# Silu in halves and two gates at earlier places in a four-layer Mamba stage

## The chip, the cores and the metric

One core of one Trainium2 chip. The metric is device microseconds of one execution of the whole kernel. Three runs of the kernel before gave 6634.72, 6636.77 and 6638.04 us, median 6636.77.

## The reference, cut to what matters

The kernel is a chain of eight stages: self-attention, cross-attention, feed-forward, a Mamba stage, a norm, cross-attention, feed-forward and a last attention. Only the Mamba stage is changed. It works on 8 sequences of 576 positions (64 of a prefix, 512 of the input) with 256 channels, in four layers of this block:

```
xi, z = split(x @ ip_w.T, 2)                  # 512 channels each
xi = silu(causal depthwise conv of 4 taps(xi) + cb)
dt, Bm, Cm = split(xi @ xp_w.T, [16, 32])     # 16 + 16 + 16
dt = softplus(dt @ dtp_w.T + dtp_b)
dA = exp(dt * A);  dBu = dt * Bm * xi         # 512 channels x 16 states
h = dA * h + dBu  (over the positions);  y = sum over states of h * Cm
y = (y + xi * D) * silu(z)
out = y @ op_w.T  (+ residual)
```

## The kernel before, in words

The 8 x 576 positions are one row of 4608, cut into 9 chunks of 512. Four layers of 9 chunks make 36 **steps** (a loop over 2 of 18 bodies; N is the body, c the chunk). A step scans 512 channels x 16 states = 8192 rows, 128 at a time: 64 **units** (i = 0 to 63) of 128 x 512, two to a **pair** (j = 0 to 31), eight pairs to a channel group k of 128 channels.

What each engine does for a pair, every one in a program order written out by hand:

- POOL (GpSimd) makes the fed product u * B for both units (line 2506). For ten pairs (0, 5, 8, 11, 14, 16, 20, 24, 26, 28) it also multiplies the scanned state with C (line 2511), three pairs later. After pair 26 and pair 31 it makes dt * xi for the next step (line 2252) and writes a reset value (line 2255).
- ACT (ScalarE) saves the last state column of pair j - 2 (line 2133, or line 2129 for a pair of POOL's), once that pair's PSUM slots have been read, and then writes exp(dt * A) into the slots (line 2474). There are four slots, two pairs.
- DVE (VectorE) scans each unit (line 2429) and, for the 22 pairs that POOL does not take, multiplies with C, one instruction for each unit (line 2237).
- PE (TensorE) folds the states of a pair into the bank of its channel group (line 2384), and signals `summed`.

Between these stand the pieces that prepare the next step, each at a fixed unit or pair: on PE the conv-and-input projections of channel groups 0 to 3 at pairs (23, 25), (27, 28), (30, 31) and, one step on, (2, 3) (project_x, line 1992), the output projection at pairs 5 and 6 (lines 2032 to 2043), the mean square at pair 7 (line 2018), the x projection at pairs 10 and 11 (line 2052), dt at 15 and 19, z at 13, 21, 24, 29 (line 2010). On ACT the copies out of PSUM, Square behind unit 5 (line 2205), silu of all of z behind unit 7 (lines 2168 and 2169), bias of group 3 behind unit 13 (line 2161), silu of all of xi behind unit 15 (lines 2173 and 2174), residual copies behind units 18 and 19 (lines 2146 and 2143), Ln and Exp of the norm behind 21 and 23 (lines 2208, 2211), softplus behind 37 and 45. Each silu is a load of the silu table, one 128 x 2048 activation, and a load of the exp table. On DVE the **gates**, y * silu(z) for one channel group (line 2232): group 3 of the step before ahead of unit 7, groups 0, 1, 2 ahead of units 23, 39 and 55. Gate k waits for `summed` of pair 8k + 7.

PE comes to a piece or a fold only after all that stands ahead of it. DVE comes to the scan of a unit only after the gate that stands ahead of it. The four lines that set the places:

```
E_OUT, G_OUT, F_OUT, SILU_AT = (59, 3, 9, 13), 29, (55, 49, 33, 1), (15, 7)
SQUARE_AT, RSTD_AT, SCALE_AT = 5, (21, 23), 26
for f in range(KI - 1):
    if i == 16 * (f + 1) + 7: gate(e, N, f, z[:, n % 2])
```

Of the kernel before, what the change touches and what calls it, by code (L numbers as in the profile page):

```python
# [18 lines left out]
ALU = mybir.AluOpType  # L19
ACT = mybir.ActivationFunctionType  # L20
# [1803 lines left out]
def load_first(e, core, layer):  # L1824

    e.dma_start(core.weights[1][:, CONV_AT:CONV_AT + TAPS * KD * DI], layer_of(core.taps, layer)).then_inc(core.first_loaded, 16)
    e.dma_start(layer_vec(core, "norm", "conv_b"), vec_from(core, layer, "norm", "conv_b")).then_inc(core.first_loaded, 16)
# [44 lines left out]
def val(N, per, off):  # L1872

    l, j = N
    return l * (BODIES * per) + (j * per + off)
# [14 lines left out]
def v_at(N, name):  # L1890

    return BEFORE_V[name] + 1 if N[1] == -2 else val(N, len(LANE_V), V_BASE + LANE_V[name] + 1)


def s_at(N, name):

    return BEFORE_S[name] + 1 if N[1] == -2 else val(N, len(LANE_S), S_BASE + LANE_S[name] + 1)
# [12 lines left out]
def mamba(core):  # L1910
    at = 0
    ring, at = core.area(at, RING, 2, TC)
# [5 lines left out]
    u, at = core.area(at, KI, TC)  # L1918
# [59 lines left out]
    def reset_of(c):  # L1978

        return 64 * (c % CHUNKS) if c % CHUNKS < B else None  # L1980
# [40 lines left out]
    def late_pe(e, N, j, c, xi, nb, gone):  # L2021

        if j == E_AT[3][0]:
            e.wait_ge(ln.v_free, v_before(N, "E3"))
        for half in range(2):
            if j == E_AT[3][half]:
                project_x(e, 3, half, c + 1, lane_v, nb, ln.v_full)
        if j == PE_B[1]:
            if N[1] >= 0:
                e.wait_ge(gated, gated_at(previous(N), KI - 1))  # L2030
            if N[1] >= 0:
                e.matmul(ybank[1], core.ident[:], chunk(c + CHUNKS - 1)[:, 1, :], start=True, stop=False)
                for k in range(KI):
                    mm = e.matmul(ybank[1], out_w[:, k, P:D], gone[:, k, :], start=False, stop=(k == KI - 1))
            else:
                mm = e.matmul(ybank[1][:, 0:2], core.ident[:], core.ident[:, 0:2], start=True, stop=True)
            mm.then_inc(y_full, 1)
        if j == PE_B[0]:
            e.wait_ge(ln.s_free, s_before(N, "B0"))
            if N[1] >= 0:  # L2040
                e.matmul(lane_s, core.ident[:], chunk(c + CHUNKS - 1)[:, 0, :], start=True, stop=False)
                for k in range(KI):
                    mm = e.matmul(lane_s, out_w[:, k, 0:P], gone[:, k, :], start=False, stop=(k == KI - 1))
            else:
                mm = e.matmul(lane_s[:, 0:2], core.ident[:], core.ident[:, 0:2], start=True, stop=True)
            mm.then_inc(ln.s_full, 1)
        if j == G_AT[0]:
            e.wait_ge(ln.s_free, s_before(N, "G"))
            e.wait_ge(silu, val(N, 2, 4))
        if j in G_AT:  # L2050
            for k in (0, 1) if j == G_AT[0] else (2, 3):
                mm = e.matmul(lane_s[0:48, :], x_w[:, k, :], xi[:, k, :], start=(k == 0), stop=(k == KI - 1))
            if j == G_AT[1]:
                mm.then_inc(ln.s_full, 1)
        for pair in range(2):
            if j == PE_H[pair]:
                project_dt(e, N, pair)
        if j == PE_F[2]:
            if N[1] >= 0:
                e.wait_ge(gated, gated_at(N, 0))  # L2060
            project_z(e, N, 2, ybank[0], nb).then_inc(y_full, 1)
        if j == PE_F[1]:
            if N[1] >= 0:
                e.wait_ge(gated, gated_at(N, 1))
            else:
                e.wait_ge(y_added, 1)
            project_z(e, N, 1, ybank[1], nb).then_inc(y_full, 1)
        if j == PE_F[0]:
            e.wait_ge(ln.v_free, v_before(N, "F0"))
            project_z(e, N, 0, lane_v, nb).then_inc(ln.v_full, 1)  # L2070
        if j == PE_F[3]:
            if N[1] >= 0:
                e.wait_ge(gated, gated_at(N, 2))
            else:
                e.wait_ge(y_free, 1)
            project_z(e, N, 3, ybank[0], nb).then_inc(y_full, 1)
# [29 lines left out]
            e.wait_ge(y_free, y_free_at(N, "F1"))  # L2106
        e.matmul(ybank[k % 2], diag[:, k, :], xi[:, k, :], start=True, stop=False)

    E_OUT, G_OUT, F_OUT, SILU_AT = (59, 3, 9, 13), 29, (55, 49, 33, 1), (15, 7)
    H_OUT = (37, 45)  # L2110

    def soft_plus(e, N, pair):
# [35 lines left out]
    def late_act(e, N, n, i, c, xi, zi, zn):  # L2148

        if i == F_OUT[3] and N[1] >= 0:  # L2150
            e.wait_ge(y_full, y_at(previous(N), "F3"))
            e.activation(zn[:, 3, :], ybank[0], ACT.Copy).then_inc(y_free, 1)
        if i == E_OUT[1]:
            e.wait_ge(ln.v_full, v_at(previous(N), "E1"))
            e.activation(xi[:, 1, :], lane_v, ACT.Identity, bias=lv("conv_b", 1)).then_inc(ln.v_free, 1)
        if i == E_OUT[2]:
            e.wait_ge(ln.s_full, s_at(previous(N), "E2"))
            e.activation(xi[:, 2, :], lane_s, ACT.Identity, bias=lv("conv_b", 2)).then_inc(ln.s_free, 1)
        if i == E_OUT[3]:
            e.wait_ge(ln.v_full, v_at(N, "E3"))  # L2160
            e.activation(xi[:, 3, :], lane_v, ACT.Identity, bias=lv("conv_b", 3)).then_inc(ln.v_free, 1)
        if i == SILU_AT[1]:
            if N[1] >= 0:
                e.wait_ge(y_free, y_free_at(N, "F3"))
                e.wait_ge(ln.v_free, v_at(previous(N), "F0"))
            else:
                e.wait_ge(cleared, 1)
            e.activation(zn, zn, ACT.Silu).then_inc(silu, 1)
            e.preload_act_table_set("natural_log_exp_and_others")
        if i == SILU_AT[0]:  # L2170
            e.wait_ge(ln.v_free, v_at(N, "E3"))
            e.wait_ge(ln.s_free, s_at(previous(N), "E2"))
            e.activation(xi, xi, ACT.Silu).then_inc(silu, 1)
            e.preload_act_table_set("natural_log_exp_and_others")
        for m in range(KD):
            if i == RESIDUAL[m]:
                residual(e, N, m, c)
        if i == G_OUT:
            e.wait_ge(ln.s_full, s_at(N, "G"))
            if N[1] >= 0:  # L2180
                e.wait_ge(bc_stored, val(N, 16, 16))
            e.activation(xdbl[0:48, :], lane_s[0:48, :], ACT.Copy).then_inc(ln.s_free, 1)
        for pair in range(2):
            if i == H_OUT[pair]:
                e.preload_act_table_set("softplus")
                soft_plus(e, N, pair)
                e.preload_act_table_set("natural_log_exp_and_others")
        if i == F_OUT[2]:
            e.wait_ge(y_full, y_at(N, "F2"))
            e.activation(zi[:, 2, :], ybank[0], ACT.Copy).then_inc(y_free, 1)  # L2190
        if i == F_OUT[1]:
            e.wait_ge(y_full, y_at(N, "F1"))
            e.activation(zi[:, 1, :], ybank[1], ACT.Copy).then_inc(y_free, 1)
        if i == F_OUT[0]:
            e.wait_ge(ln.v_full, v_at(N, "F0"))
            e.activation(zi[:, 0, :], lane_v, ACT.Copy).then_inc(ln.v_free, 1)

    SQUARE_AT, RSTD_AT, SCALE_AT = 5, (21, 23), 26

    def early_act(e, N, i, c, xe, nb, nb_before):  # L2200

# [25 lines left out]
    def gate(e, N, k, zi):  # L2227

        e.wait_ge(summed, summed_at(N, SP_ * (k + 1) - 1))
        if k == 0:  # L2230
            e.wait_ge(silu, val(N, 2, 3))
        e.tensor_tensor(zi[:, k, :], ybank[k % 2], zi[:, k, :], ALU.mult).then_inc(gated, 1)

    def times_c(e, N, n, j, h):
# [12 lines left out]
    def times_x(e, N, pair, xi, c):  # L2247

        e.wait_ge(ln.s_free, s_at(N, ("H0", "H3")[pair]))
        e.wait_ge(ln.v_free, v_at(N, ("H1", "H2")[pair]))  # L2250
        at = slice(2 * pair, 2 * pair + 2)
        e.tensor_tensor(u[:, at, :], dt[:, at, :], xi[:, at, :], ALU.mult).then_inc(u_done, 1)
        e.wait_ge(u_done, u_done_at(N, pair, 1))
        p = reset_of(c)
        e.tensor_tensor(scrap[:, 12:14] if p is None else dt[:, at, p], far, core.one[:, 0:2], ALU.mult).then_inc(u_done, 1)

    def build_diag(e):

# [26 lines left out]
    with core.nc.Block() as block:  # L2285
        @block.sync
        def _(e):
# [12 lines left out]
            for l in range(LAYERS // 2):  # L2300
                for j in range(BODIES):
# [9 lines left out]
                    spread_dt(e, 2)  # L2311
                    spread_u(e, 2)
                    if c == CHUNKS - 2:
                        load_first(e, core, after)
                    store_bc(e, N, (j + 1) % 2)
                    e.wait_ge(scanned, scanned_at(N, 31))
# [77 lines left out]
        def _(e):  # L2394
# [15 lines left out]
            for l in range(LAYERS // 2):  # L2410
                for n in range(BODIES):
                    N, c = (l, n), n % CHUNKS
                    layer = l * 2 + n // CHUNKS
                    for i in range(UN):
# [3 lines left out]
                            e.wait_ge(core.first_loaded, layer * FIRST_LOAD + 2 * FIRST_LOAD)  # L2418
                        early_dve(e, N, i, c, normed[:, n % 2])
                        for f in range(KI - 1):  # L2420
                            if i == 16 * (f + 1) + 7:
                                gate(e, N, f, z[:, n % 2])
                        if i == 7:
                            gate(e, previous(N), KI - 1, z[:, (n + 1) % 2])
# [404 lines left out]
```

## Time and profile before

| | |
|---|---|
| median of 3 runs | 6636.77 us |
| profiled execution, its time / its span | 6639.8 / 6638.0 us |
| Mamba scans, first to last | 2054.0 to 5993.9 us of the span |
| busy share of the span: PE, DVE, ACT, POOL | 92%, 74%, 55%, 66% |
| mean granted TensorE clock | 0.941 |

Read it like this: the shares are means over eight stages. In the Mamba stage, 59% of the span, DVE's row of the slices shows 9 in every slice, POOL's too, PE's 8 or 9 and ACT's 6. The page's chain of work that ended last covers only the last stages, so the Mamba stage is read from timelines.

### The profile page before, as it was taken

The numbers are of one execution on the slowest core, as the hardware profiler recorded it, in microseconds if no ns is written. First come the engines' busy times: TensorE is split into PE (matmuls) and PEld (weight loads), VectorE is DVE, ScalarE is ACT, GpSimd is POOL, SyncE is SP. The second block draws the span as 40 slices with busy tenths as digits, with TensorE's granted clock in tenths as the row PEclk, the third lists the DMA queues.
The fourth block names the chain that finished last, engine by engine and source line by source line (L and its number), as shares of the span: only waits on it lengthen the run. The fifth ranks groups of instructions, "written<-read, shape, count | busy, mean of one in ns | idle before, by whom it ended". The sixth has DMA issues, their size and how long they took to land. (4 is left out here: it accounts for less than half of the span.)

```text
span 6638.0 us, 60681 instructions
## 1 busy us (share of the span) xinstructions
PE 6129.0 (92%) x20586; PEld 2577.4 (39%) x20586; DVE 4928.1 (74%) x5709; ACT 3620.5 (55%) x6605; POOL 4394.1 (66%) x2056
## 2 busy tenths in 40 slices
PE   9999999999999989898899989898989898988898
PEld 4555555544443333323333323333323343323444
DVE  4444445543225999999999999999999999995623
ACT  4444445432225666666666666666666666664432
POOL 3333334323005999999999999999999999992300
PEclk9999999999998989899989999999999898989998
DMA  2000000213002333333333333332333232332000
GB/s 80 1 1 1 1 1 1 86 26 102 20 0 68 83 76 78 78 93 85 72 89 71 83 88 86 71 89 65 89 81 93 65 89 65 93 80 56 4 0 26
DMA packets 228678, 387.64 MB, mean 58 GB/s; under 512 B 46304, under 2 KB 64416, under 8 KB 225936
## 3 DMA queue, kind: packets, MB, share of 16 engines
q1 hardware_dynamic: 228368, 383.75, 23.7%
q8 instruction: 164, 2.69, 0.2%
q14 instruction: 146, 1.20, 0.1%
HBM read 207.14 MB, written 23.40 MB: 35 GB/s over the span
## 5 line engine op out<-in xcount | busy, mean ns | idle before, releaser
L2506 POOL TENSOR_TENSOR work<-work,weights 128x1024 f32<-128x1024 f32 x1152 | 2685.6, 2361 | 15.8 <-PE banks L2384 6.8
L2429 DVE TENSOR_TENSOR_SCAN banks<-banks,work 128x512 f32<-128x512 f32 x1584 | 1985.7, 1272 | 53.5 <-ACT banks L2474 48.1
L2384 PE MATMUL banks<-work 128*64 128x512 f32 x4608 | 1353.9, 670 | 378.2 <-POOL work L2511 271.1
L2474 ACT ACTIVATE banks<-work 128x512 f32<-128x512 f32 x2304 | 1496.0, 680 | 25.5
L1992 PE MATMUL banks<-work,weights 128*128 128x512 f32 (+31 forms) x3796 | 1140.6, 451 | 3.0 <-DVE work L2222 3.0
L2237 DVE TENSOR_TENSOR work<-banks,weights 128x512 f32<-128x512 f32 x1584 | 1056.0, 668 | 0.0
L2511 POOL TENSOR_TENSOR work<-work,weights 128x1024 f32<-128x1024 f32 x360 | 848.0, 2356 | 238.4 <-ACT work L2129 238.4
L2429 DVE TENSOR_TENSOR_SCAN work<-banks,work 128x512 f32<-128x512 f32 x720 | 911.2, 1269 | 99.8 <-ACT banks L2474 97.2
L603 POOL TENSOR_TENSOR work<-work 128x1024 f32<-128x1024 f32 x256 | 479.6, 1893 | 743.4 <-DVE work L470 742.9
L1992 PEld LDWEIGHTS banks<-work,weights 128*128 128x128 f32 x3796 | 634.4, 190 | 600.0 <-issue 523.6
L2133 ACT ACTIVATE work<-banks 128x2 f32<-128x2 f32 x792 | 135.9, 172 | 1227.4 <-DVE work L2237 1225.6
L2384 PEld LDWEIGHTS banks<-work 128*64 128x64 f32 x4608 | 271.0, 145 | 1236.4 <-issue 500.8
L553 ACT ACTIVATE work<-banks,work 128x512 f32<-128x512 f32 x512 | 347.7, 690 | 201.1 <-DVE work L464 201.1
L464 DVE TENSOR_REDUCE work<-banks 128x2 f32<-128x1024 f32 x256 | 308.8, 1214 | 105.1 <-PE banks L389 104.7
L2010 PE MATMUL banks<-work,weights 128*128 128x512 f32 x592 | 350.7, 722 | 0.0
L1040 PE MATMUL banks<-work,weights 128*128 128x512 f32 x768 | 341.5, 599 | 9.4 <-ACT work L215 9.4
L454 DVE COPY work<-banks 128x512 f32<-128x512 f32 x256 | 175.5, 685 | 160.3 <-PE banks L379 160.3
L379 PE MATMUL banks<-ident,work 128*128 128x128 f32 x2048 | 277.9, 279 | 8.2 <-DVE work L454 4.6
L379 PEld LDWEIGHTS banks<-ident,work 128*128 128x128 f32 x2048 | 222.1, 141 | 151.7 <-issue 111.1
L389 PE MATMUL banks<-work 64*128 64x512 f32 x1024 | 254.4, 615 | 0.0
L366 PE MATMUL banks<-work 128*64 128x256 f32 x2048 | 247.5, 385 | 0.0
L322 PE MATMUL banks<-work,weights 128*128 128x512 f32 x512 | 224.9, 597 | 6.4 <-ACT work L215 4.2
(312 smaller groups left out, 6796.9 us busy)
## 6 DMA issues: line engine op xcount, KB each, us to landing
weights<-mamba_bc SPq DMA_DIRECT2D x592, 256.0 KB, 5.0
work<-work SPq DMA_DIRECT2D x1160, 128.0 KB, 2.3
weights<-mamba_taps SPq DMA_DIRECT2D x5, 2048.0 KB, 7.5
weights<-cross_vo SPq DMA_DIRECT2D x16, 512.0 KB, 6.9
mamba_taps<-work SPq DMA_DIRECT2D x4, 2048.0 KB, 7.8
cross_vo<-weights SPq DMA_DIRECT2D x6, 1024.0 KB, 8.4
work<-in_conv_rows SPq DMA_DIRECT2D x16, 256.0 KB, 6.7
out_T<-X SPq DMA_DIRECT2D x8, 512.0 KB, 3.3
```

The costliest lines, as they stand in the source:

```text
L379: mm = e.transpose(core.banks[:, 4 + j, kt * P:(kt + 1) * P], probs[:, 2 * (g % 2) + u, j, kt * P:(kt + 1) * P], core.ident[:])
L553: last = e.activation(probs[:, slot, j, :], core.banks[:, 2 * u + j, :], ACT.Exp, bias=nmax[:, slot, j:j + 1], accum_out=sums[:, slot, j:j ...
L603: e.tensor_tensor(probs[:, slot], probs[:, slot], rsum[:, slot, :].unsqueeze(2).to_broadcast([P, 2, T]), ALU.mult) \
L1040: mm = e.matmul(bank(i), w1[:, k, m * P:(m + 1) * P], normed[:, k, :], start=(k == 0), stop=(k == KD - 1))
L1992: mm = e.matmul(lane[:, a:b], conv_w[j][:, k, m * P:(m + 1) * P], nb[:, k, a + j:b + j], start=(d == 0 and k == 0), stop=(j == 0 and b == ...
L2010: mm = e.matmul(lane, z_w[:, k, m * P:(m + 1) * P], nb[:, k, TAPS - 1:], start=(k == 0), stop=(k == KD - 1))
L2237: last = e.tensor_tensor(ring_pair(n, j)[:, h, :], banks[:, slot_of(i), :], bc[:, j % SP_, 1, :], ALU.mult)
L2384: mm = e.matmul(ybank[k % 2][64 * h:64 * h + 64, :], fold, ring_pair(n, j)[:, h, :], start=False, stop=(a == SP_ - 1))
L2429: e.tensor_tensor_scan(ub if by_pool(j) else da, da, ub, state[:, i:i + 1], ALU.mult, ALU.add).then_inc(scanned, 1)
L2474: e.activation(banks[:, slot_of(i), :], dt_rep[:, k % 2, h, :], ACT.Exp, scale=decay[:, f:f + 1]).then_inc(da_full, 1)
L2506: e.tensor_tensor(ring_pair(n, j), u_rep[:, k % 2], bc[:, a, 0, :].unsqueeze(1).to_broadcast([P, 2, TC]), ALU.mult) \
L2511: e.tensor_tensor(ring_pair(n, q), ring_pair(n, q), bc[:, q % SP_, 1, :].unsqueeze(1).to_broadcast([P, 2, TC]), ALU.mult) \
```

## The change

Places of work on ACT and DVE move inside the step; ACT's two silus of 2048 columns become four of 1024. z is done in halves behind units 5 and 27, xi behind units 15 and 21, each half with its own two table loads. The bias of group 3 moves from 13 to 15 (ahead of the first xi half), Ln and Exp from 21 and 23 to 23 and 24. Gates 0 and 1 move from 23 and 39 to 21 and 37; gate 2 stays at 55, and gate 3 at 7. PE's x projection waits for the second xi half. POOL's small reset write is left out where there is no reset (one step in nine). SP waits for the group 3 bias before it loads the next layer's first weights (once a layer). The change's own short title also names VectorE's products with C, "one for each unit"; the diff has no line of `times_c`, which makes one for each unit already.

```diff
@@ late_pe
         if j == G_AT[0]:
             e.wait_ge(ln.s_free, s_before(N, "G"))
-            e.wait_ge(silu, val(N, 2, 4))
+            e.wait_ge(silu, val(N, 4, 7))
@@
-    E_OUT, G_OUT, F_OUT, SILU_AT = (59, 3, 9, 13), 29, (55, 49, 33, 1), (15, 7)
+    E_OUT, G_OUT, F_OUT = (59, 3, 9, 15), 29, (55, 49, 33, 1)
+    Z_SILU, X_SILU = (5, 27), (15, 21)
+    GATE_AT = (21, 37, 55)
@@ late_act
-        if i == SILU_AT[1]:
...
-            e.activation(zn, zn, ACT.Silu).then_inc(silu, 1)
-            e.preload_act_table_set("natural_log_exp_and_others")
-        if i == SILU_AT[0]:
...
-            e.activation(xi, xi, ACT.Silu).then_inc(silu, 1)
-            e.preload_act_table_set("natural_log_exp_and_others")
+        for half in range(2):
+            at = slice(2 * half, 2 * half + 2)
+            if i == Z_SILU[half]:
...
+                e.activation(zn[:, at, :], zn[:, at, :], ACT.Silu).then_inc(silu, 1)
+                e.preload_act_table_set("natural_log_exp_and_others")
+            if i == X_SILU[half]:
...
+                e.activation(xi[:, at, :], xi[:, at, :], ACT.Silu).then_inc(silu, 1)
+                e.preload_act_table_set("natural_log_exp_and_others")
@@
-    SQUARE_AT, RSTD_AT, SCALE_AT = 5, (21, 23), 26
+    SQUARE_AT, RSTD_AT, SCALE_AT = 5, (23, 24), 26
@@ gate
-        if k == 0:
-            e.wait_ge(silu, val(N, 2, 3))
+        if k % 2 == 0:
+            e.wait_ge(silu, val(N, 4, (5, 8)[k // 2]))
@@ times_x
+        p = reset_of(c)
+        e.tensor_tensor(u[:, at, :], dt[:, at, :], xi[:, at, :], ALU.mult).then_inc(u_done, 2 if p is None else 1)
+        if p is None:
+            return
@@ sync
                     if c == CHUNKS - 2:
+                        e.wait_ge(ln.v_free, v_at(N, "E3"))
                         load_first(e, core, after)
@@ vector
-                            if i == 16 * (f + 1) + 7:
+                            if i == GATE_AT[f]:
```

## Rows read from the trace of the kernel before

**Rows 1.** Stretches: length, busy us (x) of PE, PEld, DVE, ACT, POOL, PE clock, DMA.

```profile
3359.00:3408.50 49.50, 49.50 (x171) 23.62 (x171) 46.44 (x51) 34.92 (x60) 44.95 (x21) 1.00 0.46 107
2054.00:5994.00 3940.00, 3561.79 (x10573) 1301.16 (x10571) 3808.31 (x4103) 2535.20 (x4505) 3684.90 (x1662) 0.92 0.35 81
```

**Rows 2.** Waits of DVE, 2070 to 5995 us: total, times, longest.

```profile
DVE work L2429 <- ACT banks L2474: 71.5, 36, 2.4
DVE banks L2429 <- ACT banks L2474: 41.7, 40, 1.2
DVE work L2232 <- PE banks L2384: 4.1, 7, 1.0
```

**Rows 3.** Timeline of DVE: start, us, line; units 41, 6, 8, 16, 21, gate 0, 38, 41.

```profile
3333.61 1.27 DVE L2429 TENSOR_TENSOR_SCAN work<-banks,work 128x512 f32<-128x512 f32 x1
...
3379.87 1.27 DVE L2429 TENSOR_TENSOR_SCAN banks<-banks,work 128x512 f32<-128x512 f32 x1
...
3385.24 1.29 DVE L2429 TENSOR_TENSOR_SCAN banks<-banks,work 128x512 f32<-128x512 f32 x1 [1.14 <-ACT banks L2474]
...
3400.26 1.28 DVE L2429 TENSOR_TENSOR_SCAN work<-banks,work 128x512 f32<-128x512 f32 x1 [1.92 <-ACT banks L2474]
...
3407.95 1.28 DVE L2429 TENSOR_TENSOR_SCAN banks<-banks,work 128x512 f32<-128x512 f32 x1
...
3411.50 0.68 DVE L2232 TENSOR_TENSOR work<-banks,work 128x512 f32<-128x512 f32 x1
...
3436.60 1.29 DVE L2429 TENSOR_TENSOR_SCAN banks<-banks,work 128x512 f32<-128x512 f32 x1
...
3442.53 1.27 DVE L2429 TENSOR_TENSOR_SCAN work<-banks,work 128x512 f32<-128x512 f32 x1
```

**Rows 4.** Timeline of POOL: products with C of pairs 20 and 26.

```profile
3335.43 2.35 POOL L2511 TENSOR_TENSOR work<-work,weights 128x1024 f32<-128x1024 f32 x1 [1.00 <-ACT work L2129]
...
3356.51 2.36 POOL L2511 TENSOR_TENSOR work<-work,weights 128x1024 f32<-128x1024 f32 x1
```

**Rows 5.** Timeline of PE: fold 26, output projection, fold 7.

```profile
3358.92 1.08 PE L2384 MATMUL banks<-work 128*64 128x512 f32 x4 [0.52 <-POOL work L2511]
...
3400.97 3.60 PE L2043 MATMUL banks<-work,weights 128*128 128x512 f32 x8
...
3407.43 1.08 PE L2384 MATMUL banks<-work 128*64 128x512 f32 x4
```

**Rows 6.** Timeline of ACT in the same step.

```profile
3373.84 1.29 ACT L2474 ACTIVATE banks<-work 128x512 f32<-128x512 f32 x2
...
3375.16 1.05 ACT L2205 ACTIVATE work<-X 128x1024 f32<-128x1024 f32 x1
...
3379.73 1.28 ACT L2168 ACT_TABLE_LOAD   x1
3381.02 1.91 ACT L2168 ACTIVATE work<-work 128x2048 f32<-128x2048 f32 x1
...
3384.25 0.17 ACT L2133 ACTIVATE work<-banks 128x2 f32<-128x2 f32 x1
3384.45 1.30 ACT L2474 ACTIVATE banks<-work 128x512 f32<-128x512 f32 x2
...
3392.75 0.69 ACT L2161 ACTIVATE work<-banks,weights 128x512 f32<-128x512 f32 x1 [0.55 <-PE banks L1992]
...
3404.61 0.60 ACT L2143 ACTIVATE X<-banks 128x512 f32<-128x512 f32 x1 [0.45 <-PE banks L2043]
...
3405.20 1.29 ACT L2474 ACTIVATE banks<-work 128x512 f32<-128x512 f32 x2
```

**Rows 7.** Timeline of ACT and PE ahead of the first scan.

```profile
2020.19 0.69 ACT L2161 ACTIVATE work<-banks,weights 128x512 f32<-128x512 f32 x1 [6.17 <-PE banks L1992]
...
2031.06 0.59 ACT L2182 ACTIVATE work<-banks 48x512 f32<-48x512 f32 x1 [4.25 <-PE banks L2052]
...
2025.69 5.33 PE L2052 MATMUL banks<-work,weights 128*48 128x512 f32 x8 [2.78 <-ACT work L2143]
```

More of the change, by code:

```diff
@@ L2161, in late_act @@
             e.activation(xi[:, 3, :], lane_v, ACT.Identity, bias=lv("conv_b", 3)).then_inc(ln.v_free, 1)
-        if i == SILU_AT[1]:
[L2163 to L2167, printed above, removed]
-            e.activation(zn, zn, ACT.Silu).then_inc(silu, 1)
-            e.preload_act_table_set("natural_log_exp_and_others")
-        if i == SILU_AT[0]:
-            e.wait_ge(ln.v_free, v_at(N, "E3"))
-            e.wait_ge(ln.s_free, s_at(previous(N), "E2"))
-            e.activation(xi, xi, ACT.Silu).then_inc(silu, 1)
-            e.preload_act_table_set("natural_log_exp_and_others")
+        for half in range(2):
+            at = slice(2 * half, 2 * half + 2)
+            if i == Z_SILU[half]:
+                if half == 0 and N[1] >= 0:
+                    e.wait_ge(y_free, y_free_at(previous(N), "F1"))
+                    e.wait_ge(ln.v_free, v_at(previous(N), "F0"))
+                if half == 0 and N[1] < 0:
+                    e.wait_ge(cleared, 1)
+                if half == 1 and N[1] >= 0:
+                    e.wait_ge(y_free, y_free_at(N, "F3"))
+                e.activation(zn[:, at, :], zn[:, at, :], ACT.Silu).then_inc(silu, 1)
+                e.preload_act_table_set("natural_log_exp_and_others")
+            if i == X_SILU[half]:
+                if half == 0:
+                    e.wait_ge(ln.v_free, v_at(previous(N), "E1"))
+                else:
+                    e.wait_ge(ln.v_free, v_at(N, "E3"))
+                    e.wait_ge(ln.s_free, s_at(previous(N), "E2"))
+                e.activation(xi[:, at, :], xi[:, at, :], ACT.Silu).then_inc(silu, 1)
+                e.preload_act_table_set("natural_log_exp_and_others")
         for m in range(KD):
@@ L2251, in times_x @@
         at = slice(2 * pair, 2 * pair + 2)
-        e.tensor_tensor(u[:, at, :], dt[:, at, :], xi[:, at, :], ALU.mult).then_inc(u_done, 1)
+        p = reset_of(c)
+        e.tensor_tensor(u[:, at, :], dt[:, at, :], xi[:, at, :], ALU.mult).then_inc(u_done, 2 if p is None else 1)
+        if p is None:
+            return
         e.wait_ge(u_done, u_done_at(N, pair, 1))
-        p = reset_of(c)
-        e.tensor_tensor(scrap[:, 12:14] if p is None else dt[:, at, p], far, core.one[:, 0:2], ALU.mult).then_inc(u_done, 1)
+        e.tensor_tensor(dt[:, at, p], far, core.one[:, 0:2], ALU.mult).then_inc(u_done, 1)
     def build_diag(e):
@@ L2313, in _ @@
                     if c == CHUNKS - 2:
+                        e.wait_ge(ln.v_free, v_at(N, "E3"))
                         load_first(e, core, after)
```

## The prediction, made blind

> **What bounds the kernel now.** I read the busy shares first, then DVE's waits, then the four engines' timelines over one step, because shares hide who waits in which part of it. In the Mamba stage DVE is busy for 3808 of 3940 us, POOL 3685, PE 3562 and ACT 2535 [rows 1]. Nearly all of DVE's idle time is a wait for ACT's exp: 71.5 and 41.7 us [rows 2]. The timeline places it. Behind unit 7 stands the silu of z, and the scan of unit 8 comes 1.22 us late, start against start; behind unit 15 stands the silu of xi, and unit 16 comes 1.99 us late [rows 3]. Both repeat in all 36 steps. The softplus behind unit 37 makes unit 38 late by 0.14 us. Read so, the stage is DVE's work plus about 3.4 us of ACT's stalls in a step of 108.92 us (scan of unit 41 to the same scan a step later [rows 3]).
>
> That isn't the whole loop. Follow PE. The scan of unit 41 starts at 3333.61. ACT saves its state, POOL, which had waited for that, makes the product of pair 20 at 3335.43, and then works without a gap to the product of pair 26, 3356.51 to 3358.87 [rows 3, 4]. PE had waited 0.52 us for this, folds pair 26 at 3358.92, and from there has no idle time at all until the fold of pair 7 ends at 3407.43 + 1.08 = 3408.51 [rows 5]: 49.50 of 49.50 us busy, at a granted clock of 1.00, which is 2.4 GHz, so nothing is left to speed up there [rows 1]. The conv and output projections stand in that run. So PE is some three pairs behind DVE at the start of a step. The end of group 3's projection is what ACT waits for ahead of unit 14 (0.55 us, until 3392.75), and behind that come the exps of pair 7, the xi silu and the late unit 16 [rows 6]. So the long stall at unit 16 is partly PE's lateness, passed on by ACT. The closed loop of today is: unit 41, POOL, PE's run, ACT, unit 16, DVE to unit 41. The trace bears this out: fold 7 ends 0.55 us behind the start of unit 21 in 33 of 36 steps, although the steps' own lengths vary from 108.9 to 114.8 us. In the step shown that is 3408.51 against 3407.95 [rows 3, 5].
>
> **The change, part by part.** All times are those of the step shown.
>
> *z half behind unit 5.* Today the two loads and the silu take 3384.25 - 3379.73 = 4.52 us; the silu itself is 1.91 us. No row shows a silu of 1024 columns. Its bounds are half of 1.91, 0.96, and all of it, 1.91; I take 1.04, the mean of the 1024-column Square [rows 6]. So a half costs 4.52 - 1.91 + 1.04 = 3.65 us. Behind the exps of pair 2 (end 3375.13) it runs to 3378.80, history copy and Square (0.09 + 1.05, now behind it) to 3379.95, the state copy 0.20, and a scan follows its exp's start by 0.79 (3384.45 to 3385.24): unit 6 starts at 3380.94, not 3379.87, 1.07 late. Unit 8 is no longer late: exps follow at once. Net at unit 8: 0.15 us earlier than today.
>
> *Bias and xi half behind unit 15.* The bias no longer stands ahead of the exps of pair 7. These end at about 3393.44, the bias at 3394.13, the half at 3397.78, and unit 16 starts at 3398.77. DVE would be there at 3398.12: 0.65 us late instead of 1.99. Unit 16 comes 1.49 us sooner than today.
>
> *Residual behind unit 19, unchanged.* It waits for PE's output projection, whose end at 3400.97 + 3.60 = 3404.57 the change does not move. Exps of pair 10 start at 3405.20 as today, so unit 20 can't start before 3405.99. DVE, ready at 3404.69, waits 1.3 us. Of the 1.49 us won, 0.19 are left.
>
> *Gate 0 ahead of unit 21.* Today it starts at 3411.50, 2.99 us behind the end of fold 7. Two scans and two products, 3.55 us (3411.50 - 3407.95), are what lies between the old place and the new. There DVE is ready at 3407.76 and fold 7 ends at 3408.51. Gate 0 waits until about 3408.56, 0.61 us later than DVE stands at this point today. Everything behind it on DVE waits too.
>
> *xi half behind unit 21.* The exps of pair 10 end at 3406.49, the half at 3410.16, exp of unit 22 starts at 3410.36, its scan at 3411.15. DVE arrives at 3408.56 + 0.60 + 1.19 + 0.59 = 3410.94: 0.21 late. With 0.96 for the half it would be 0.13, with 1.91 it would be 1.08. Offset against today: 0.61 + 0.21 = 0.82 us. PE's x projection finds this half done by 3407.9, long before fold 9, so its new wait costs nothing.
>
> *Ln and Exp behind 23 and 24, z half behind 27.* The exps of units 24 and 25 are then ready about 0.1 us ahead of their scans: nothing. Behind 27 ACT has its slots early, since pair 11 is POOL's, and between unit 23 and unit 28 DVE has two norm products more: ready some 0.8 us early. Nothing; if that cover goes, the half's excess over DVE's work lands on unit 28.
>
> *Gate 1 ahead of 37.* Its 0.60 us now cover the softplus: unit 38's 0.14 us go [rows 3]. Fold 15 ends at the start of unit 37 in 17 steps (up to 2 us sooner in the others), so it may wait 0.05 there. I book -0.14.
>
> *The rest.* POOL's small write goes in 8 places: under 0.2 us each. SP's wait is over before SP gets there (unit 15's scan, then the bias a few us on): nothing but a later load, used a step and a half on. The products with C are one for each unit already: nothing. The four more table loads and the longer silus, 5.3 us of ACT in a step, otherwise lie in ACT's idle time, (3940 - 2535) / 36 = 39 us a step [rows 1].
>
> *Ahead of the first scan* nothing is hidden. From the end of the group 3 bias at 2020.88: first half 3.65, two tiny copies, table and silu of the second half until 2027.0; the x projection (5.33 us, began at 2025.69) ends at about 2032.4; ACT meanwhile does the second load, Ln, Exp and the last z half until 2033.2, so the copy of dt, B and C starts there and not at 2031.06 [rows 7]. +2.2 us.
>
> **The sum.** In a step 0.82 - 0.14 = +0.68 us, with no other slack in the loop to take it: unit 41 starts later by this, and with it POOL, PE's run and the next gate 0. 36 x 0.68 = 24.5; three steps have fold 7 0.17 to 0.3 us sooner, -0.5; +2.2. In all +26 us: 6666 us against the profiled execution's 6639.8, which lies 3 us above the median; against the median, 6663 us. What this kernel's measurement can tell from no change is about 0.2%, 13 us.
>
> A rule speaks against the change more strongly: every switch of table set costs 2.66 us with its drain, so work should be grouped by set (the Trainium skill, "ScalarE: Activation LUTs", What ACT_TABLE_LOAD costs). The rows disagree on the size, since two loads and the silu between them take 4.52 us in all [rows 6]; by the page the sum would be that of the last rival.
>
> **The rivals.**
>
> *Faster: PE doesn't hold gate 0 or the residual.* If PE's run came along with DVE, only ACT's stalls would count: 1.22 + 1.99 + 0.14 today, 1.07 + 0.65 + about 0.2 changed, 1.4 us less a step, 36 x 1.4 = 51, less 2.2 ahead of the first scan: 6588 us. For it: DVE's waits name ACT for 113 us and PE for 4 [rows 2]. Against it: a run of 49.5 us without idle time that starts from unit 41, and the constant 0.55 us. Chance 0.15.
>
> *Same: the two small terms are smaller.* The ends of matmuls are modelled. If fold 7 is readable 0.3 us sooner and the half is 0.96, the step gains 0.61 - 0.3 + 0.13 - 0.14 = 0.3: 36 x 0.3 + 2.2 = 13 us at most, 6645 us. Against it: gate 3, which waits for fold 31, never starts less than 0.05 us behind its modelled end. Chance 0.14.
>
> *Slower by more: a half-size silu is hardly shorter.* At 1.91 unit 22 is 1.08 late: 36 x 0.87 = 31 us more, 6694 us. It decides from 0.83 us on, where the half outlasts gate, scan and product. Against it: all other ACT rows grow with their columns. Chance 0.04.
>
> *Slower by far: a switch costs twice its load.* Then a half takes 3.65 + 2 x 1.28 = 6.2 us, nearly all of the difference lands on unit 22 and some on unit 16: about +3.2 us a step, 6752 us. This is that page's rule as a mechanism of this kernel. Against it: the 4.52 us. Chance 0.01.
>
> **How the numbers follow.** The forecast, PE-bound gate 0, has 0.66 and its own range is 6652 (no late unit 22) to 6675 (half of 1.3 us). Slower by over 0.2%: 0.66 + 0.04 + 0.01 = 0.71; same 0.14; faster 0.15. The range goes from 6630, which takes in the same case with some gain ahead of it, to 6678; it leaves out the faster rival and the two dear ones, 0.20.
>
> **What the changed profile would show.** DVE's waits name PE ahead of gate 0 in nearly every step, about 0.8 us each, some 25 to 30 us in all against 4.1. ACT's waits remain: about 1.0 at unit 6, 0.6 at 16, 1.2 at 20 (behind the residual, so PE's), 0.2 at 22; none at 8 and 38. The step is 109.6 us, PE's run from fold 26 to fold 7 still 49.6 us without a gap, table loads 8 + 4 a step. I am wrong if gate 0 starts without a wait, if the silu halves differ from 1.04 us, or if PE's run is shorter: then the loop was not through PE.

## The result and the profile after

| | before | changed |
|---|---|---|
| median of 7 runs each | 6636.85 us | 6661.6 us |
| ratio, 95% interval | | 1.004 (1.0028 to 1.0051) |
| profiled execution's span | 6638.0 us | 6664.4 us |
| first scan / last scan start | 2054.0 / 5992.7 us | 2058.2 / 6021.5 us |
| scan of unit 41 to the same a step later, mean of 35 | 109.32 us | 110.01 us |

Slower by 0.4%: +0.69 us a step. One of the seven runs of the kernel before, at 7251.69 us where the others lie between 6632.89 and 6638.04, is left out of the ratio. Lines 2429, 2384, 2232, 2237, 2506, 2511 and 2474 of before are 2441, 2396, 2241, 2246, 2518, 2523 and 2486 now. The first view is again DVE's list of waits over the Mamba stage (total us, times, longest):

```profile
DVE banks L2441 <- ACT banks L2486: 87.0, 71, 1.9
DVE work L2241 <- PE banks L2396: 24.7, 36, 0.7
DVE work L2441 <- ACT banks L2486: 22.3, 37, 1.3
DVE work L2441 <- POOL work L2518: 2.8, 3, 0.9
```

The sum named ACT went from 113 us [rows 2] to 109; what is new is the line with PE, 36 times, once a step. The timeline of DVE in the step that answers to the one shown before (units 6, 16, 20, gate 0, units 21, 22; all starts are 12.26 us later than in that trace, counted at the scan of unit 41 ahead of it, 3345.87 against 3333.61):

```profile
3393.13 1.29 DVE L2441 TENSOR_TENSOR_SCAN banks<-banks,work 128x512 f32<-128x512 f32 x1 [0.91 <-ACT banks L2486]
...
3410.84 1.28 DVE L2441 TENSOR_TENSOR_SCAN work<-banks,work 128x512 f32<-128x512 f32 x1 [0.46 <-ACT banks L2486]
...
3418.26 1.29 DVE L2441 TENSOR_TENSOR_SCAN banks<-banks,work 128x512 f32<-128x512 f32 x1 [1.42 <-ACT banks L2486]
...
3420.83 0.69 DVE L2241 TENSOR_TENSOR work<-banks,work 128x512 f32<-128x512 f32 x1 [0.70 <-PE banks L2396]
3421.43 1.28 DVE L2441 TENSOR_TENSOR_SCAN banks<-banks,work 128x512 f32<-128x512 f32 x1
...
3423.44 1.28 DVE L2441 TENSOR_TENSOR_SCAN work<-banks,work 128x512 f32<-128x512 f32 x1
```

Units 8 and 38 wait no more, unit 16 waits 0.46 where it waited 1.92 [rows 3]. Up to there DVE has won 1.68 us (unit 16 at 3410.84 - 12.26 = 3398.58 against 3400.26). Not all of it is the half silu's. These lines of ACT are the first xi load and the next instruction behind the block, first before, then changed:

```profile
3394.74 1.28 ACT L2173 ACT_TABLE_LOAD   x1
...
3399.26 0.17 ACT L2133 ACTIVATE work<-banks 128x2 f32<-128x2 f32 x1
```

```profile
3406.18 1.28 ACT L2182 ACT_TABLE_LOAD   x1
...
3409.84 0.17 ACT L2135 ACTIVATE work<-banks 128x2 f32<-128x2 f32 x1
```

The block takes 3.66 us instead of 4.52, which is 0.86; and it starts 0.82 us sooner (3406.18 - 12.26 = 3393.92 against 3394.74), because the group 3 bias, which before waits for PE until 3392.75 [rows 6], no longer stands ahead of the exps of pair 7.

Then three waits behind one another, at unit 20, gate 0 and unit 22, take it all back and more. (Unit 22 starts 0.82 us behind the start of the product ahead of it, where 0.59 is usual, so it is 0.23 us late; the view doesn't list idle time that short.) PE and ACT in the same step say why:

```profile
3413.25 3.60 PE L2043 MATMUL banks<-work,weights 128*128 128x512 f32 x8
3416.78 1.08 PE L2396 MATMUL banks<-work 128*64 128x512 f32 x4
3417.78 1.99 PE L2018 MATMUL banks<-work,mean_d 128*128 128x512 f32 x4
3419.70 1.08 PE L2396 MATMUL banks<-work 128*64 128x512 f32 x4
```

```profile
3416.88 0.60 ACT L2145 ACTIVATE X<-banks 128x512 f32<-128x512 f32 x1 [2.15 <-PE banks L2043]
3417.38 0.20 ACT L2131 ACTIVATE work<-work 128x2 f32<-128x2 f32 x1
3417.47 1.29 ACT L2486 ACTIVATE banks<-work 128x512 f32<-128x512 f32 x2
3418.78 1.28 ACT L2182 ACT_TABLE_LOAD   x1
3420.08 1.06 ACT L2182 ACTIVATE work<-work 128x1024 f32<-128x1024 f32 x1
3421.15 1.28 ACT L2183 ACT_TABLE_LOAD   x1
3422.44 0.17 ACT L2135 ACTIVATE work<-banks 128x2 f32<-128x2 f32 x1
```

PE's output projection ends at 3416.85, the residual copy waits 2.15 us for it where it waited 0.45 [rows 6], and behind it come the exps of pair 10, the second xi half, and unit 22. Fold 7 ends at 3419.70 + 1.08 = 3420.78, and gate 0 starts 0.05 us later. In this step PE did nothing else than before: its fold of pair 7 starts 73.83 us behind the scan of unit 41 (3419.70 - 3345.87), 73.82 before (3407.43 - 3333.61, [rows 3, 5]). Over 35 steps the end of fold 7 lies 74.92 us behind that scan in the middle (median), 74.90 before; 30 of the steps agree within 0.05 us, and in five the fold is 0.15 to 0.28 us sooner now. Fold 7 to unit 21 of the same step: unit 21 started 0.55 us ahead of fold 7's end in 33 of 36 steps before, and 0.65 us behind it in all 36 now.

### The profile page after: what moved, and what is told of

Its sections match the earlier page's. It is cut to its first block and busy times, and to the rows that moved or that the text cites. A ratio compares the mean times of both kernels' runs of the same rounds, so it can differ in the third digit from the quotient of the medians.

```text
span 6664.4 us, 60931 instructions
## 1 busy us (share of the span) xinstructions
PE 6131.3 (92%) x20586; PEld 2566.7 (39%) x20586; DVE 4933.8 (74%) x5709; ACT 3821.4 (57%) x6827; POOL 4397.1 (66%) x2048
## 5 line engine op out<-in xcount | busy, mean ns | idle before, releaser
L2396 PE MATMUL banks<-work 128*64 128x512 f32 x4608 | 1322.3, 667 | 403.6 <-POOL work L2523 284.1
L2396 PEld LDWEIGHTS banks<-work 128*64 128x64 f32 x4608 | 257.3, 144 | 1272.0 <-issue 475.2
```

Of the source, the lines that this page charges most:

```text
L2396: mm = e.matmul(ybank[k % 2][64 * h:64 * h + 64, :], fold, ring_pair(n, j)[:, h, :], start=False, stop=(a == SP_ - 1))
```

## Experiments

Two theories were tested first. **P**: the loop of a step goes through PE's run, which holds DVE in two ways, by fold 7 for gate 0, and by the output projection for the residual copy, the exps of pair 10 and what stands behind them. **A**: the time went to ACT, for four more table loads a step and new places of the silus. Ratios are to the kernel before on the same chip.

### Gate 0 sooner, alone (g0_only)

```diff
# kernel before
-                            if i == 16 * (f + 1) + 7:
+                            if i == (21, 39, 55)[f]:
```

> The kernel before with one edit: gate 0 ahead of unit 21 instead of 23. Theory P (the loop of a step goes through PE, and fold 7 holds gate 0): gate 0 starts 0.05 us behind fold 7's end, 0.61 us later than DVE stands there, 36 x 0.61 = 22 us slower, 6659 us, ratio 1.0033. Rival A (the time was lost to ACT: four more table loads and the new places of the silus): no change, 6637 us.

Measured: 6662.47 us, ratio 1.0039 (1.0025 to 1.0053). One integer of the whole change, alone, costs as much as the whole change does; P had 22 us, 27 were measured (0.60 us a step in the trace, which is 22). DVE's waits of this run:

```profile
DVE work L2429 <- ACT banks L2474: 71.5, 36, 2.4
DVE banks L2429 <- ACT banks L2474: 41.6, 40, 1.1
DVE work L2232 <- PE banks L2384: 22.1, 43, 1.0
```

The two lines with ACT are those of [rows 2] to 0.1 us; PE's went from 4.1 to 22.1 us. The gate starts 0.05 us behind fold 7 in all 36 steps. A, by which this edit would cost nothing, can't explain the loss here; that the table loads aren't a part of it is shown further down, by the runs that keep them.

### Gate 0 back, the rest changed (g0_back)

```diff
# changed kernel
-    GATE_AT = (21, 37, 55)
+    GATE_AT = (23, 37, 55)
```

> The changed kernel with gate 0 back ahead of unit 23. Theory P, with the residual copy that waits for PE as second holder: the xi half behind unit 21 ends at the same time, unit 22 starts at 3411.15 in the frame of the step shown before (about 1.6 us late), and gate 0 comes behind it: +1.42 - 0.14 = +1.28 us a step against the kernel before, with 3 us ahead of the first scan 6686 us, slower than the change. Rival B (the wait ahead of gate 0 is the whole loss): it goes, 0.8 us a step less than the change, 6634 us. Rival A: as the change, 6662 us.

Measured: 6684.16 us, ratio 1.0071 (1.0058 to 1.0084). So the sooner gate is not a mistake to be undone by itself: beside a silu behind unit 21 its 0.60 us cover part of the silu. The wait has gone to unit 22:

```profile
3424.79 1.29 DVE L2441 TENSOR_TENSOR_SCAN banks<-banks,work 128x512 f32<-128x512 f32 x1 [1.42 <-ACT banks L2486]
...
3429.98 1.28 DVE L2441 TENSOR_TENSOR_SCAN work<-banks,work 128x512 f32<-128x512 f32 x1 [1.53 <-ACT banks L2486]
```

These are units 20 and 22, 5.19 us apart as in the changed kernel (3418.26 to 3423.44, 5.18), with the gate now behind them. Rival B falls.

### Each holder alone (c8, res22)

```diff
# c8: changed kernel, mean square behind fold 7
-    G_AT, PE_B, PE_C, PE_H, PE_F = (10, 11), (6, 5), 7, (15, 19), (24, 21, 13, 29)
+    G_AT, PE_B, PE_C, PE_H, PE_F = (10, 11), (6, 5), 8, (15, 19), (24, 21, 13, 29)
# res22: changed kernel, residual copy of group 0 behind unit 22
-    RESIDUAL = (19, 18)
+    RESIDUAL = (22, 18)
```

> The changed kernel with the mean square at pair 8, so behind fold 7, and nothing else. This takes one of the two holders of theory P away (fold 7 for gate 0) and leaves the other (residual copy, exps of pair 10, xi half, unit 22). Theory P: gate 0 starts when DVE gets there, at 3407.76 of the step shown before, unit 22 still starts at 3411.15 and waits about 1.0 us: the same time as the change, 6662 us. Rival B (the gate's wait is the loss): 0.6 to 0.8 us a step less, 6633 to 6640 us.

Measured: 6660.77 us, ratio 1.0033 (1.002 to 1.0046).

> The changed kernel with the residual copy of group 0 behind unit 22 and nothing else: the other holder taken away. Theory P: unit 20 and unit 22 no longer wait, gate 0 waits about 2.1 us for fold 7 and starts at 3408.56 as in the change; the offset is 0.61 - 0.14 = 0.47 us a step, 6637 + 17 + 3 = 6657 us. Rival C (the residual copy is the loss): its 1.5 us at unit 20 come back, 6610 us.

Measured: 6656.54 us, ratio 1.0026 (1.0016 to 1.0036). The same two places of DVE's timeline in each, first c8 (units 20 and 22), then res22 (gate 0):

```profile
3415.14 1.29 DVE L2441 TENSOR_TENSOR_SCAN banks<-banks,work 128x512 f32<-128x512 f32 x1 [1.42 <-ACT banks L2486]
...
3420.32 1.28 DVE L2441 TENSOR_TENSOR_SCAN work<-banks,work 128x512 f32<-128x512 f32 x1 [0.94 <-ACT banks L2486]
```

```profile
3417.82 0.69 DVE L2241 TENSOR_TENSOR work<-banks,work 128x512 f32<-128x512 f32 x1 [2.21 <-PE banks L2396]
```

In c8 gate 0 no longer waits and unit 22 waits 0.94 instead; in res22 units 20 and 22 no longer wait and gate 0 waits 2.21 instead of 0.70. Two holders stand side by side, and either alone keeps most of the loss: 23 us of the change's 25 in c8, 19 in res22 (medians, against the kernel before on the same chip). Rival B had 6633 to 6640 us for c8 and rival C 6610 us for res22, so both fall.

### Both holders away (res22_g23, res22_c8)

```diff
# res22_g23: changed kernel
-    RESIDUAL = (19, 18)
+    RESIDUAL = (22, 18)
-    GATE_AT = (21, 37, 55)
+    GATE_AT = (23, 37, 55)
# res22_c8: changed kernel, the two edits of c8 and res22
```

> The changed kernel with the residual copy of group 0 behind unit 22 instead of 19, and gate 0 ahead of 23. All halves and table loads stay. Theory P: nothing ahead of gate 0 waits for PE's run any more except gate 3; gate 0 finds fold 7 done 1.5 us before; the stalls left are 1.07 (unit 6), 0.65 (unit 16), 0.14 (unit 46), so a step is 107.3 us, 1.6 less than before: 6637 - 57 + 3 = 6583 us. Rival A: the table loads are still there, 6655 to 6665 us.

Measured: 6585.61 us, ratio 0.9925 (0.9913 to 0.9937).

> The changed kernel with the residual copy of group 0 behind unit 22, gate 0 still ahead of 21, and the mean square (1.9 us of PE) at pair 8 instead of 7, so behind fold 7. Theory P: fold 7 ends 1.9 us sooner in PE's run, gate 0 starts 1.3 us before where DVE stood in the kernel before: -1.3 - 0.14 a step, 6637 - 52 + 3 = 6588 us. Rival A: 6655 to 6665 us, since ACT's and DVE's work is that of the change.

Measured: 6585.57 us, ratio 0.9922 (0.9909 to 0.9934). Two different ways out of PE's run, the same 76 us below the change, with every half and every table load in place. A had 6655 to 6665 us for both, and falls. One miss in each: in res22_g23 unit 22 is still 0.41 us late, probably by the group 1 residual copy, which stands ahead of the exps of pair 10 (moving it was not tried); in res22_c8 gate 0 still comes 0.2 to 0.3 us late, by fold 7, in most steps.

### Is it the residual alone? (before_res22)

```diff
# kernel before
-    RESIDUAL = (19, 18)
+    RESIDUAL = (22, 18)
```

> The kernel before with the residual copy of group 0 behind unit 22, whole silus and all gates as before. Are the halves worth anything by themselves, or is the residual the whole of the 50 us? Theory P: unit 16 is held by group 3's bias and the whole xi silu, unit 8 by the z silu, neither of them by the residual: 6635 to 6640 us, no change. Rival C: 6590 to 6610 us.

Measured: 6638.59 us, ratio 1.0 (0.9991 to 1.0009). In the kernel before the residual holds nothing; the whole silus and the group 3 bias, at the places they had, hold units 8 and 16 without it, so rival C falls again. The rest of the change is therefore worth 50 us, but only once PE's run doesn't hold what comes behind. How much of the 50 us is the halves' no run separates, since the bias and gate 1 have moved too: at unit 16 the lines of ACT above give 0.86 us to the half silu and 0.82 to the bias's new place, in the step shown.

### A version made from this (apart, apart_c7, apart_g39)

```diff
# apart: changed kernel
-    E_OUT, G_OUT, F_OUT = (59, 3, 9, 15), 29, (55, 49, 33, 1)
+    E_OUT, G_OUT, F_OUT = (59, 3, 9, 17), 29, (55, 49, 33, 1)
-    SQUARE_AT, RSTD_AT, SCALE_AT = 5, (23, 24), 26
+    SQUARE_AT, RSTD_AT, SCALE_AT = 11, (23, 24), 26
-    RESIDUAL = (19, 18)
+    RESIDUAL = (22, 18)
-    GATE_AT = (21, 37, 55)
+    GATE_AT = (23, 37, 55)
-    G_AT, PE_B, PE_C, PE_H, PE_F = (10, 11), (6, 5), 7, (15, 19), (24, 21, 13, 29)
+    G_AT, PE_B, PE_C, PE_H, PE_F = (10, 11), (6, 5), 8, (15, 19), (24, 21, 13, 29)
# apart_c7: apart, and
-    G_AT, PE_B, PE_C, PE_H, PE_F = (10, 11), (6, 5), 8, (15, 19), (24, 21, 13, 29)
+    G_AT, PE_B, PE_C, PE_H, PE_F = (10, 11), (6, 5), 7, (15, 19), (24, 21, 13, 29)
# apart_g39: apart_c7, and
-    GATE_AT = (23, 37, 55)
+    GATE_AT = (23, 39, 55)
```

> A version made from theory P: halves as changed, gate 0 ahead of 23, residual copy behind 22, mean square at pair 8, group 3's bias behind 17 (off the path of the first xi half), Square behind 11 (not beside the first z half). Theory P: units 6 and 16 wait no more either, a step is DVE's work plus 0.14 and what PE and POOL then hold: 105.6 to 106.3 us, 6637 - 3.0 x 36 + 3 = 6532 us (6520 to 6545). If POOL's chain or PE's run holds it sooner than I work out, 6545 to 6575 us, with POOL or PE named ahead of a scan or a gate.

Measured: 6542.32 us, ratio 0.9853 (0.984 to 0.9867), in the range, 10 us above its middle. Units 6 and 16 wait no more (unit 6 in 5 steps of 36), but two waits are left, units 22 (36 steps) and 24 (30 steps). The moves of the bias, of Square and of the mean square were made together, so the time doesn't tell what each is worth. The two waits:

```profile
3374.56 1.28 DVE L2441 TENSOR_TENSOR_SCAN work<-banks,work 128x512 f32<-128x512 f32 x1 [0.33 <-ACT banks L2486]
...
3378.48 1.29 DVE L2441 TENSOR_TENSOR_SCAN banks<-banks,work 128x512 f32<-128x512 f32 x1 [0.27 <-ACT banks L2486]
```

The second comes from ACT's Ln, which now waits for the mean square moved to pair 8:

```profile
3376.90 0.66 ACT L2217 ACTIVATE banks<-banks,eps 128x512 f32<-128x512 f32 x1 [1.35 <-PE banks L2018]
```

> The version of the run before with the mean square back at pair 7. In that run ACT's Ln waits 1.35 us for the mean square at pair 8, and unit 24 is 0.35 us late behind it. With gate 0 ahead of 23 there are 2.2 us between fold 7 and the gate, so the 1.9 us of the mean square fit ahead of fold 7. Theory P: unit 24's wait goes, gate 0 starts 0.3 us behind fold 7 without a wait, 36 x 0.4 = 14 us less: 6528 us. If fold 7 now holds gate 0: 6540 us or more, with PE named ahead of the gate.

Measured: 6544.08 us, ratio 0.9857 (0.984 to 0.9873): a miss. Unit 24's wait went as expected and fold 7 didn't hold gate 0 (it waits in 7 steps only), but 21.8 us of DVE's waits in the Mamba stage name PE, 16.6 of them at gate 1, which now waited up to 0.71 us for fold 15 in 30 steps. The prediction had booked gate 1 ahead of unit 37 as having no room; in this sum it was forgotten.

> The run before with gate 1 back ahead of unit 39. There unit 24's wait had gone, but gate 1, ahead of 37, waited 0.67 us for fold 15 in most steps. Theory P: two units later gate 1 has 3 us of room, its wait goes, the softplus stall of 0.14 us at unit 38 comes back: 36 x 0.5 = 18 us less than the run before, 6526 us. Rival D (PE or POOL as a whole now set the step, and a wait taken away at one gate comes back at the next): within 5 us of the run before, 6540 to 6548 us, with PE or POOL named at another place.

Measured: 6531.9 us, ratio 0.984 (0.9826 to 0.9853), 107 us below the kernel before's 6638.56 on the same chip, the fastest of all. Rival D falls: the waits at gate 1 are gone and most of what they cost doesn't come back elsewhere. The step is 0.39 us shorter than in the run before, where 0.5 was expected; unit 38 is late by about 0.16 us again. DVE's waits in the Mamba stage of this run:

```profile
DVE work L2441 <- ACT banks L2486: 12.7, 36, 0.7
DVE work L2241 <- PE banks L2396: 5.2, 14, 0.5
DVE work L2441 <- POOL work L2518: 2.7, 3, 0.9
DVE banks L2441 <- ACT banks L2486: 1.8, 4, 0.5
```

```profile
2054.00:5890.00 3836.00, 3518.48 (x10560) 1300.18 (x10559) 3802.38 (x4101) 2727.89 (x4720) 3681.11 (x1652) 0.92 0.35 83
```

DVE is now busy for 3802 of 3836 us (columns as in [rows 1]). The 34 us between the two are an estimate of what is left to win by order alone; the next step has to take work off DVE.

## Why the prediction was right

- **The loop through PE.** It was read from two things: a run of PE without idle time that began from DVE's unit 41, and a distance between fold 7 and unit 21 that did not vary when the step did. PE's part is the same to 0.01 us in both kernels in the step shown, and g0_only shows the hold by itself. The waits naming PE came to 24.7 us, just under the 25 to 30 written down.
- **Gate 0, 0.61 us.** Counted from unit 41's scan, gate 0 starts at 3420.83 - 12.26 = 3408.57 in the frame of before; 3408.56 was written down.
- **Unit 22, 0.21 us.** 3423.44 - 12.26 = 3411.18 against 3411.15. The half silu took 1.06 us, for which 1.04 was taken from a Square of the same size.
- **Units 6 and 16.** 3380.87 and 3398.58 against 3380.94 and 3398.77: late by 1.00 and 0.54 in the step shown, where 1.07 and 0.65 were worked out. Neither reaches the sum, since unit 20 waits for the residual anyway (3406.00 against 3405.99).
- **The softplus stall at unit 38** went, as booked.
- **Per step** 0.69 us against 0.68. Three slips on the way there don't reach the sum: the stall at unit 8 stands at 0.95 to 1.23 us in 32 of the 36 steps and at 0.11 to 0.47 in the other four, not in all alike; the small-terms rival's 13 us come to 6650 us, not 6645; and without the late unit 22 the forecast's own range would begin at 6655, not 6652.
- **Ahead of the first scan** was the term that was mis-sized: 4.2 us against 2.2. From the bias of group 3 to the copy of dt, B and C it is 13.59 us now and was 10.87, so 2.7 us are lost in between, 0.5 more than worked out. ACT alone would have lost 2.37 us: it was ready 0.35 us before the copy started. It is PE that ends this stretch, not ACT: the x projection took 6.43 us where 5.33 was assumed. That goes with the clock and needs no halves: the granted clock was 0.56 over those 6.43 us and 0.68 over the 5.33, and in before_res22, with whole silus, the same projection took 6.38 us at 0.56.

```profile
2021.67 0.69 ACT L2163 ACTIVATE work<-banks,weights 128x512 f32<-128x512 f32 x1 [6.17 <-PE banks L1992]
...
2035.26 0.59 ACT L2191 ACTIVATE work<-banks 48x512 f32<-48x512 f32 x1 [0.35 <-PE banks L2052]
...
2028.79 6.43 PE L2052 MATMUL banks<-work,weights 128*48 128x512 f32 x8 [4.39 <-ACT work L2182]
```

  The other 1.5 us stand ahead of the bias, where the change does next to nothing: PE's mean granted clock from 1985 to 2020 us was 0.91 before and 0.83 now. Behind the last scan the changed execution is 2.4 us shorter than the other (642.9 against 645.3 us), which hid the error in the profiled executions' difference. That is luck; no cause was looked for, and that stretch lies anywhere from 638.8 to 645.3 us in the twelve traces. The front edge moves too: the first scan came at 2051.8 in g0_only, which changes nothing ahead of it, at 2054.0 in the kernel before, and at 2055.1 and 2057.2 in c8 and g0_back, which stand there as the changed kernel does.
- **The rivals.** "PE doesn't hold" gave 6588 us; that is nearly the time of the two kernels in which PE was kept from holding, 6586 us. So its arithmetic was nearly right and its condition false. The rival of the dear switch is not borne out either: a load took 1.28 us, and from the start of the first load to the next instruction behind the second it is 3422.44 - 3418.78 = 3.66 us for two loads and the half silu. The Trainium skill gives 2.66 us for every switch of set, 1.28 for the load and the rest for a drain ("ScalarE: Activation LUTs", What ACT_TABLE_LOAD costs). The trace agrees on the load and shows no drain on top of it.

## What to carry to other kernels

A stall named "waits for ACT" may be another engine's lateness passed on: look for an engine that has no idle time at all between two points of the step, and for a distance between two engines that stays constant while the step's length varies. Where work is moved sooner on one engine, ask first how much room the result it needs has there; here it had 2.99 us and the move took 3.55. And when a step has two holders side by side, taking one away shows almost nothing, so test them together before a part is called worthless: with both in place the change stood 25 us above the kernel before, with both away 50 us below it.

## What the runs showed that was not expected

Two things. The timing repeats so exactly from step to step (gate 0 at 0.05 us behind fold 7 in 36 of 36 steps, the fold itself, in the step shown, within 0.01 us of its place in another kernel's trace) that a place two units off is visible in a 6.6 ms kernel. And the gain of order alone was larger than the change's own idea: with halves, gate 0 and gate 1 at their old places, and bias, Square and residual moved off the silus, the time is 1.6% below the kernel before.
